# Recurrent block with sliding-window attention on one core: gate's low parts, the broadcast rows, the last stores of y and the last row tile are rearranged

## The reference

```python
B, T, C = 4, 1024, 1024
xn = layernorm(x)                                     # eps 1e-5
# attention: causal band of 512 plus 4 sink columns
q, k, v = xn @ Wq.T, xn @ Wk.T, xn @ Wv.T
att = softmax(mask(q k^T / 8)); y = att @ v
s = y @ Wo.T
# feed-forward
x_norm = layer_norm(xn, in_gamma, in_beta)            # eps 1e-6
thought = x_norm[:, -1, :] @ agg_w + agg_b
for _ in range(4):
    t = gelu(layer_norm(thought, pn_gamma, pn_beta) @ d1_w + d1_b)
    thought = thought + (t @ d2_w + d2_b)
broadcast = (thought @ bc_w + bc_b)[:, None, :]
gate = sigmoid(xn @ gate_w + gate_b)
g = silu(layer_norm(xn + gate * broadcast, out_gamma, out_beta))
out = x + s * g
```

## Time and profile before

| what | us |
| --- | --- |
| three runs | 2213.40, 2222.34, 2224.83 (median 2222.34) |
| the profiled execution | 2214.79 |
| its span, from the first to the last instruction | 2213.02 |
| TensorE busy | 2148.7 |
| VectorE busy | 1446.0 |
| ScalarE busy | 868.3 |
| GpSimd busy | 263.9 |
| mean granted TensorE clock | 0.994 of full |

### The profile page before, as it was taken

How to read it: one execution, slowest core, us unless ns; L and a number is a source line. 1 busy time by engine, 2 the same in 40 slices (tenths; PEclk the granted TensorE clock), 3 DMA queues, 4 the chain that set the end, 5 groups by cost and what they waited for, 6 DMA issues and landing times. The chain is left out here.

```text
span 2213.0 us, 35988 instructions
## 1 busy us (share of the span) xinstructions
PE 2148.7 (97%) x13433; PEld 1603.0 (72%) x13433; DVE 1446.0 (65%) x3233; ACT 868.3 (39%) x1817; POOL 263.9 (12%) x542
## 2 busy tenths in 40 slices
PE   7999999999999999999999999979999999999997
PEld 6677667766676767666676666658888888888886
DVE  6466676575666656567647565665767676776777
ACT  2354565444555535455535455452111111111111
POOL 2100111010002120011201000140000101010100
PEclk9999999999999999999999999999999999999999
DMA  7496469434448633545944446636242424233331
GB/s 258 144 282 216 138 206 308 160 126 133 146 165 280 208 134 127 184 140 194 295 159 130 148 143 205 230 105 223 101 152 104 142 104 152 102 144 116 131 138 52
DMA packets 174386, 366.59 MB, mean 166 GB/s; under 512 B 13321, under 2 KB 111881, under 8 KB 159905
## 3 DMA queue, kind: packets, MB, share of 16 engines
q1 hardware_dynamic: 168240, 348.30, 46.9%
q0 software_dynamic: 5568, 14.79, 2.0%
q10 hardware_dynamic: 432, 1.57, 0.2%
HBM read 284.79 MB, written 79.72 MB: 165 GB/s over the span
## 5 line engine op out<-in xcount | busy, mean ns | idle before, releaser
L1044 PE MATMUL j_ps<-x_hi,w 128*128 128x512 f32 x1232 | 409.4, 402 | 0.0
L822 ACT ACTIVATE pt<-t_ps 128x512 f32<-128x512 f32 x432 | 238.0, 596 | 428.2 <-PE t_ps L1111 427.8
L831 ACT ACTIVATE probs<-probs,neg_max 128x660 f32<-128x660 f32 (+5 forms) x512 | 356.7, 703 | 53.7 <-DVE neg_max L1367 53.6
L1367 DVE CUSTOM_DVE_ANT_0 probs<-s_ps,mask 128x660 f32<-128x660 f32 (+5 forms) x512 | 322.4, 667 | 74.0 <-PE s_ps L1079 71.5
L1765 PE MATMUL out_ps<-wo,w 128*128 128x512 f32 x1536 | 353.4, 389 | 2.6 <-DVE w L1822 2.6
L1765 PEld LDWEIGHTS out_ps<-wo,w 128*128 128x128 f32 x1536 | 288.3, 188 | 62.7 <-issue 3.0
L1765 PE MATMUL gate_ps<-x_hi,w 128*128 128x512 f32 x1024 | 281.6, 391 | 4.8 <-PEq L470 4.8
L1044 PEld LDWEIGHTS j_ps<-x_hi,w 128*128 128x128 f32 x1232 | 228.9, 188 | 50.4 <-issue 3.8
L1079 PEld LDWEIGHTS s_ps<-k_hi,q 64*128 64x128 f32 x1664 | 159.8, 185 | 136.5 <-issue 78.8
L1079 PE MATMUL s_ps<-k_hi,q 64*128 64x330 f32 (+5 forms) x1664 | 251.6, 330 | 4.4 <-DVE neg_max L1367 1.6
L1111 PE MATMUL t_ps<-ident,probs 128*128 128x128 f32 x1728 | 243.0, 281 | 12.4 <-DVE x_lo L1355 5.7
(11 more groups left out here) (184 smaller groups left out, 2344.0 us busy)
## 6 DMA issues: line engine op xcount, KB each, us to landing
fw<-in_L_ffn_d_w_dram SPq DMA_DIRECT2D x128, 1024.0 KB, 5.3
w<-WT SPq DMA_DIRECT2D x36, 1024.0 KB, 5.1
w<-XS SPq DMA_DIRECT2D x64, 512.0 KB, 6.4
XS<-x_hi SPq DMA_DIRECT2D x32, 512.0 KB, 5.3
XS<-x_lo SPq DMA_DIRECT2D x32, 512.0 KB, 6.7
Y<-y SPq DMA_DIRECT2D x256, 64.0 KB, 2.5
b_x<-in_L_attn_x_dram SPq DMA_DIRECT2D x32, 512.0 KB, 4.1
b_y<-Y SPq DMA_DIRECT2D x32, 512.0 KB, 6.4
```

What stands on the lines that cost most here:

```text
L822: act.activation(pt[:, m % PT_SLOTS, :, :], bank[:, :].rearrange("p (h q) -> p h q", q=P), ACT.Copy).then_inc(pt_ready, 1)
L831: act.activation(probs[:, slot, 0:width], probs[:, slot, 0:width], ACT.Exp, bias=neg_max[:, slot:slot + 1], scale=-1.0, accum_out=row_sum[ ...
L1044: last = pe.matmul(bank_of((kind, b, n)), w[:, slot, wp * C + c * P:wp * C + c * P + P], xs[:, c, bass.ts(ch, BANK)], start=i == 0, stop=i ...
L1367: dve.tensor_tensor_reduce(out=probs[:, slot, 0:width].rearrange("p (a n) -> p a n", a=parts), in0=s_ps[head % 2][:, :].rearrange("p (a n) ...
```

## The change

- `GATE_AT`: the eight row blocks of gate fall on units 26 to 31 as 1, 2, 2, 1, 1, 1 instead of 1, 1, 1, 2, 2, 1. In GpSimd's queue `pack_sinks` now stands ahead of the low parts. The low part of the eighth block is made by VectorE, behind the last step's work and `take_y` of unit 126.
- SyncE stores the broadcast rows ahead of the stores of y of unit 126, and the stores of y of unit 127 move into `finish`, behind the second Wo load. gate_bias, the first y tile and the second x tile are loaded behind the sixth Wo block instead of the fourth.
- The last two tiles are written out by a function `last_two` on each engine. In the diff SyncE's stands first, then ScalarE's and TensorE's; VectorE's is told behind it. The last tile has other tensors as its own: `z_a` (a y tile), `z_res` (a normalised x), `z_hi` and `z_lo` (the first gate operands) and `z_ps` (the first gate result). ScalarE makes the high part of the last y as soon as these are free. TensorE makes the last output product by halves of 512 columns, all 24 matmuls of one half ahead of the other's. VectorE's order for tiles 30 and 31 is interleaved anew, and the last tile's final product, sum and store go by halves.

```diff
-        GATE_AT = {26: (0,), 27: (1,), 28: (2,), 29: (3, 4), 30: (5, 6), 31: (7,)}
+        GATE_AT = {26: (0,), 27: (1, 2), 28: (3, 4), 29: (5,), 30: (6,), 31: (7,)}
...
-                for u in range(UNITS * B - 2, UNITS * B):
-                    store_y(u)
-
                 sp.wait_ge(thought_ready, 4 + 2 * B)
                 for half in range(2):
                     sp.dma_start(BC[:, half, :], t_rows).then_inc(bc_stored, 16)
+
+                store_y(UNITS * B - 2)
                 sp.wait_ge(bc_stored, 32)
...
+                        if has_sink(unit_of(s)[1]):
+                            pack_sinks(UNITS * b + s)
+
                         if b == B - 1:
                             for k in GATE_AT.get(s, ()):
+                                if k < KB - 1:
...
-                        if has_sink(unit_of(s)[1]):
-                            pack_sinks(UNITS * b + s)
...
                 take_y(UNITS * B - 2)
+                k = KB - 1
+                dve.wait_ge(gate_high, KB)
+                dve.wait_ge(xs_stored, 32 * TB * B)
+                dve.tensor_tensor(x_lo[:, k, :], xn[k % 2], x_hi[:, k, :].bitcast(F32), ALU.subtract).then_inc(gate_split, 1)
...
+        Z = TILES - 1
+        z_a, z_res, z_hi, z_lo, z_ps = yt[0], xn[0], x_hi[0], x_lo[0], gate_ps[0]
...
-                    if n == 3:
+                    if n == 1:
+                        u = UNITS * B - 1
+                        for half in range(2):
+                            heads = head_of(unit_of(UNITS - 1)[0], 0, half) // 2
+                            sp.dma_start(Y[TILES - 1, :, heads, :].rearrange("(r d) q -> d r q", r=2),
+                                         y[u % 2][HS * half:HS * half + HS, :].rearrange("d (r q) -> d r q", q=P)
+                                         ).then_inc(y_stored[u % 2], 16)
+                    if n == RAW - 1:
                         for k in range(2):
                             sp.wait_ge(y_stored[k], 16 * B * KV * TB)
...
+                def last_two():
+                    sp.wait_ge(res_ready, after(Z))
+                    sp.dma_start(out_flat[bass.ts(Z - 1, P), :], res[:, :]).then_inc(stored, 16)
+                    for half in range(2):
+                        sp.wait_ge(res_ready, after(Z + 1 + half))
+                        part = bass.ts(half, BANK)
+                        sp.dma_start(out_flat[bass.ts(Z, P), part], z_res[:, part]).then_inc(stored, 16)
...
+                def last_two():
+                    act.wait_ge(z_ready, after(Z))
+                    act.activation(a[:, :], a[:, :], ACT.Sigmoid).then_inc(sig_ready, 1)
+                    act.wait_ge(y_loaded[1], 16 * (TILES // 2))
+                    act.wait_ge(gate_done, Z)
+                    hi_part(z_hi, yt[1], y_hi_ready)
+                    act.wait_ge(shifted, Z)
+                    act.wait_ge(stored, landed(Z - 1))
+                    act.activation(res[:, :], a[:, :], ACT.Sigmoid).then_inc(sig2_ready, 1)
+                    act.wait_ge(z_ready, after(Z + 1))
+                    act.activation(z_a[:, :], z_a[:, :], ACT.Sigmoid).then_inc(sig_ready, 1)
+                    act.wait_ge(shifted, Z + 1)
+                    act.activation(z_res[:, :], z_a[:, :], ACT.Sigmoid).then_inc(sig2_ready, 1)
...
+                def last_two():
+                    body(Z - 1, 0, Z // 2, None)
+                    pe.wait_ge(z_ready, after(Z))
+                    pe.wait_ge(y_lo_ready, after(Z + 1))
+                    for half in range(2):
+                        products(z_ps, z_hi, z_lo, parts[2], parts[3], halves=(half,)).then_inc(out_done, 1)
```

More of the change, by code:

```diff
@@ L1600, in finish @@
         wo = sb("wo", [P, O_TILES, 2, KB, P], F32R)
-        g_hi, g_lo, operands, ident, _ = shared
+        g_hi, g_lo, operands, ident, y = shared
         gate_bias, gamma, beta, bc = (sb(n, [P, C]) for n in ("gate_bias", "gamma", "beta", "bc"))
@@ L1656, in finish, with tiles @@
         GROUP = TB // 2
-        def tiles(eng, body, start=None):
+        def tiles(eng, body, start=None, last_two=None):
             with eng.Fori(0, TILES // GROUP - 1) as i:
@@ L1666, in tiles @@
                 start(TILES // GROUP - 1)
-            for s in range(GROUP):
+            for s in range(GROUP - 2 if last_two else GROUP):
                 body(TILES - GROUP + s, s % 2, (TILES - GROUP + s) // 2, TILES // GROUP - 1 if s == 0 else None)
+            if last_two:
+                last_two()
         def follows(t, n):
@@ L1716, in body @@
                     sp.dma_start(out_flat[bass.ts(t, P), :], res[:, :]).then_inc(stored, 16)
-                tiles(sp, body, load_bc)
-                sp.wait_ge(stored, landed(TILES))
+                def last_two():
[5 more added lines that the diff above has]
+                        sp.dma_start(out_flat[bass.ts(Z, P), part], z_res[:, part]).then_inc(stored, 16)
+                tiles(sp, body, load_bc, last_two)
+                sp.wait_ge(stored, landed(TILES + 1))
             @block.gpsimd
@@ L1756, in body, with products @@
                         hi_part(y_hi, yt[1 - s], y_hi_ready)
-                tiles(act, body)
+                def last_two():
[11 more added lines that the diff above has]
+                    act.activation(z_res[:, :], z_a[:, :], ACT.Sigmoid).then_inc(sig2_ready, 1)
+                tiles(act, body, None, last_two)
             @block.tensor
             def _(pe):
-                def products(out_, hi, lo, w_hi, w_lo, blocks=range(KB)):
+                def products(out_, hi, lo, w_hi, w_lo, blocks=range(KB), halves=(0, 1)):
                     for c in blocks:
                         for lhs, rhs in ((hi, w_hi), (hi, w_lo), (lo, w_hi)):
-                            for half in range(2):
+                            for half in halves:
                                 last = pe.matmul(out_[:, bass.ts(half, BANK)], lhs[:, c, :], rhs(c, half),
@@ L1801, in body @@
                     products(out_ps, y_hi, y_lo, parts[2], parts[3]).then_inc(out_done, 1)
-                tiles(pe, body)
+                def last_two():
[4 more added lines that the diff above has]
+                        products(z_ps, z_hi, z_lo, parts[2], parts[3], halves=(half,)).then_inc(out_done, 1)
+                tiles(pe, body, None, last_two)
             @block.vector
@@ L1865, in program @@
+                tiles(dve, body, None, last_two)
 def program(nc, x, Wq, Wk, Wv, Wo, in_gamma, in_beta, agg_w, agg_b, pn_gamma, pn_beta, d1_w, d1_b, d2_w, d2_b,
```

64 lines of the change are left out of this document (58 added, 6 removed).

## The result

The kernel after takes 2210.75 us (median of 9 runs, 2205.36 to 2214.89), the kernel before 2219.12 us (9 runs beside them, 2212.8 to 2224.83): ratio 0.9966, interval [0.9952, 0.9979]. The prediction was 2211.0 us.

A forecast was written before the change was run, and what follows sets the result against it. TensorE, busy 97% of the span and alone in the main loop, was taken as the bound; +2.4 - 2.7 - 1.1 - 1.1 - 5.3 = -7.8 us from a four-run mean of 2218.84 gave 2211.0 us, range 2202 to 2219.

The forecast's parts named there:

- Cost of part 1: Attention, unit 28: a second gate load makes both bc_w tiles land later, +2.4 us, bounds +2.0 to +3.4.
- the load leaves 2.4 us later: SyncE's queue, unit 28: the second gate load waits for the second GpSimd subtraction, delaying bc_w behind it by 2.4 us.
- I take 0: TensorE's clock after the bc_w waits: the existing half-clock loss of 1.7 us stays, so no change, 0.
- the +1.7 allowed for a second stretch: After the bc_w waits: a second half-clock stretch of the same length would add up to 1.7 us.
- Gain of part 1: Attention, unit 31: VectorE's merge and division no longer held up by GpSimd, -2.7 us, bounds -2.1 to -3.1.
- Crossing: Barrier into the second stage: opens earlier but GpSimd's DRAIN still holds it, -1.1 us, bounds 0 and -4.0.
- the rival in which the barrier follows VectorE: Barrier: GpSimd's DRAIN is no duration of its own, crossing gives 4.0, total 2208.1 us; chance 0.25.
- Wo's waits: Start of finish: TensorE's waits for the fifth and sixth Wo tiles go, -1.1 us, bounds -1.15 and +1.
- The clock term beside it: Start of finish: half clock in or after the wait for the first Wo load, 0 to +1.7 us, taken as 0.
- Last tile: Last tile: own buffers, VectorE's new order and a halved store end it earlier, -5.3 us, bounds -4.4 and -5.7.
- the list of signs: Expected trace signs; for the last tile, VectorE ends 12 to 13 us, not 16.7, after TensorE starts it.
- the 0.3 us for GpSimd's two small steps: Last tile: VectorE waits for GpSimd's deviation steps beside the out_ps product, 0.3 us, halfway between 0 and 0.6.

The follow-up runs named there:

- e4: Kernel after with one gate load of unit 28 moved behind the bc_w tiles instead of ahead of them; 2204.08 us, ratio 0.9948 to before.
- e13: e12 with the change's first part (GATE_AT, pack_sinks, eighth low part) undone; 2205.48 us, ratio 0.9955 to before.
- e12: e4 with GpSimd's 48 sink rows issued by SyncE, its 28 x loads kept on GpSimd; 2202.48 us, ratio 0.9925 to before.
- e5: Kernel after with one more GpSimd instruction at the end of attention, waiting for TensorE's last values; 2211.6 us, one run.
- e6: Kernel after with all GpSimd transfers in attention (x loads and sink rows) issued by ScalarE; 2226.48 us, one run.
- e10: e4 with GpSimd's 28 x loads issued by SyncE, the 48 sink rows kept on GpSimd; 2200.27 us, one run.
- e11: Kernel after with only its first part (GATE_AT, pack_sinks, eighth low part) undone; 2210.74 us, ratio 0.9958 to before.
- e8: Kernel after with the last tile's output product, last two VectorE steps and store whole instead of by halves; 2211.21 us, ratio 0.9972 to before.
- e1: Kernel before with only the new GATE_AT, pack_sinks order and eighth low part on VectorE; 2219.95 us, ratio 1.0010 to before.
- e3: Kernel before with only last_two on all engines (own buffers for the last tile, products and stores by halves); 2210.45 us, ratio 0.9972.

## Why the prediction held

**Cost of part 1: right in the pair of profiles, undersized over all kernels.** The step "the load leaves 2.4 us later" was right (2.34 us), and so was moving the landings with it (2.53). From unit 28's copy to unit 29's the pair shows +2.51 for +2.4. There "I take 0" for the clock held too: the half-clock stretch went from 3.41 to 6.83 us and covered both products, but the first product's delay is hidden by the wait for the second tile, and what is left, 0.87 + 0.63 = 1.5 us, stands against the 1.7 that before lost to its own stretch behind the second product. Not every kernel without part 1 has that loss there: over the means of five the cost is 4.2 us, and reordering the loads (e4) gains 4.2 where +2.4 stood, beyond the bound of +3.4 too; with the +1.7 allowed for a second stretch it lies inside. That before had its stretch just there was luck.

**Gain of part 1: right.** The merge and the division came down to 0.47 and 0.89 us, 2.46 of the 2.7 us, and the time from unit 29's copy to unit 30's by 2.52 us; e13 beside e12 measures 2.6 there. The eighth low part on VectorE cost nothing that the marks show. The net, forecast -0.3, is 0.00 in the pair of profiles and about +1 in the means of five; the medians say +2, within their error of zero.

**Crossing: right, and for the stated reason.** The DRAIN of 6.96 us was taken as a duration, the barrier opened at 1491.6, and the term was -1.03 for -1.1. e5 settles it against the rival in which the barrier follows VectorE. What the duration is made of was not known then.

**Wo's waits: right, the size partly by luck.** Both are gone, -1.30 for -1.1; gate_bias, y and x were in time. The clock term beside it, 0 with a bound of +1.7, was 0 here since the stretch fell ahead of the wait for the first Wo block. In e6, e10, e11 and e13, with the same order of Wo's loads, it fell behind that wait, and from TensorE's first product to the first one with Wo it took 33.14 to 34.04 us, for 33.30 before and 32.01 after: there the gain is gone.

**Last tile: -6.4 for -5.3.** Its product started with no wait at all, -2.54 for -2.3. VectorE's end is 1.1 us earlier than forecast, 0.9 of it behind the start of that product: 13.42 us, where the sum has 14.3 (2191.0 to 2205.3), although the list of signs says 12 to 13. I had put 1.26 us between any two of its steps; where a step neither reads the result of the one before nor writes over its operand, they start 1.14 us apart (2185.24, 2186.38, 2187.52), and where it reads it 1.25 (2187.52, 2188.77). And the 0.3 us for GpSimd's two small steps was not paid: beside the product of `out_ps` with a the first took 0.19 us, while beside a sum of two SBUF tiles at 2175.60 it took 1.06 again. The rule in the Trainium skill, "SBUF — State Buffer", section Who interferes with whom, is that a VectorE instruction with two SBUF inputs contends with a GpSimd one that reads SBUF, and one with at most one SBUF input does not. The trace agrees: 1.06 us and 0.19. The store gave the 0.6.

The rule in the Trainium skill, "DMA: Bandwidth & Descriptors", section Bandwidth, to batch transfers to 1 MiB or more for at least 75% of the peak, would speak for the whole store. Here the halving was no loss: e8's whole store ends 3.04 us behind VectorE's last step, the halves 2.43.

**The sum** was -7.8 us in the profiled execution, measured -9.4; of the difference 0.7 lies ahead of unit 28's copy, where I know no cause, 1.1 in the last tile and 0.2 at Wo, and part 1 took 0.3 back. The ratio's -0.34% of 2219 is -7.5 us, and its interval, -4.7 to -10.7 us, cannot tell the two sums apart. That the number on record, 2211.0, is so close to 2210.75 owes something to luck: the mean of four runs stood for before, the last tile was undersized by 1.1, and the clock, twice taken as 0, cost nothing in this pair but 1 to 2 us at each of the two places in other kernels.

## What to carry to other kernels

Before moving a load in a queue that is shared, ask which load stands behind it and who waits for that one; with one gate load moved behind two tiles that TensorE needed, part 1 went from a suggested cost of 0.1% to a gain of 0.3% (e12 beside e13). A gap on TensorE costs more than its length where half clock follows over work that nothing hides, and nothing more where TensorE then waits for a load anyway. At a barrier look at each engine's own DRAIN and subtract its last instruction; on GpSimd it grew with the number of its transfers, so many tiny ones are better issued elsewhere, or by an engine with room in its queue.

## What the runs showed of the hardware

- GpSimd's DRAIN at the end of a block took 0.73 us without transfers of its own and 0.082 us more for each that it had issued in the block (28, 48, 76: 3.04, 4.68, 6.96 us), whatever their size or age. SyncE's DRAIN, with hundreds of transfers behind it, took 0.13 to 0.14 us (0.007 in before, e1 and e3), and ScalarE's 0.63 with 3 as with 79. What makes the 0.082 us isn't shown by any row.
- Two VectorE sums or products over 128x1024 that follow without a wait started 1.13 to 1.14 us apart where the second neither read the result of the first nor wrote over its operand, and 1.25 to 1.26 where it did either. In the main loop of after these are 1.14 (the product with `out_ps` and the low part behind it), 1.13 (low part and residual) and 1.25 (residual and gate sum, which overwrites what the residual reads). A step that also waited for a sigmoid of ScalarE started at 1.21 (2184.03, 2185.24).
- The half-clock stretches between unit 26 and the main loop lasted 3.41 or 6.83 us (10.24 once, in e5, behind its gap of 6.7), and where they fell changed between executions of the same code: e11, whose code up to the crossing is that of before, has one at 1445.03 and before has none there, and the way from unit 26's copy to unit 28's is 19.50 us for 18.00. The kernel after has one there too, at 1441.29, and also takes 19.50.
